# The order in which SP's queue issues the splits' returns and the weight loads, in a two-layer gated attention kernel

## What is computed

```
x = x + tanh(g_xattn[0]) * attention0(norm(x), ctx)   # 16 heads of 8, causal mask j < i
x = x + tanh(g_ffn[0])   * experts0(norm(x))          # 6 low-rank experts, best one, log of sum of exp
x = x + tanh(g_xattn[1]) * attention1(norm(x), ctx)   # 8 heads of 64
x = x + tanh(g_ffn[1])   * experts1(norm(x))          # 2 of 8 experts per batch, GELU, norm
```

## Time and profile before

| what | us |
|---|---|
| median of 3 runs | 203.16 (201.14 to 204.28) |
| the profiled execution | 203.85 |
| its span, first to last instruction | 201.8 |

### The profile page before, as it was taken

How to read it: one execution, slowest core, us unless ns; L and a number is a source line. 1 busy time by engine, 2 the same in 40 slices (tenths; PEclk the granted TensorE clock), 3 DMA queues, 4 the chain that set the end, 5 groups by cost and what they waited for, 6 DMA issues and landing times.

```text
span 201.8 us, 4473 instructions
## 1 busy us (share of the span) xinstructions
PE 182.0 (90%) x1575; PEld 130.8 (65%) x1575; DVE 145.3 (72%) x362; ACT 121.8 (60%) x315; POOL 103.8 (51%) x152
## 2 busy tenths in 40 slices
PE   7999786698999897998999998998999999999990
PEld 2677362455556555675686775857966959989980
DVE  2466695889998865279957689498789867747674
ACT  3558412854787685679769756496779954155240
POOL 6330000248655474277871785858958846282212
PEclk9999999979999999699999999999999999999998
DMA  5788999808300000000000000000160070708010
GB/s 132 229 254 162 302 190 236 159 26 158 58 8 2 4 3 3 0 0 3 0 0 2 5 0 0 3 0 0 21 220 0 5 232 3 224 18 248 8 52 29
DMA packets 14673, 15.13 MB, mean 75 GB/s; under 512 B 1703, under 2 KB 12044, under 8 KB 14652
## 3 DMA queue, kind: packets, MB, share of 16 engines
q1 hardware_dynamic: 14292, 14.75, 28.9%
q10 hardware_dynamic: 360, 0.10, 0.3%
HBM read 11.11 MB, written 3.67 MB: 73 GB/s over the span
## 4 chain that ended last, share of the span: by engine, by line
PE 54%; DVE 19%; DMA 7%; SPq 6%; POOL 6%; issue 3%; ACT 2%; POOLq 0%; DVEq 0%; ACTq 0%
PE PS L1288 6%; PE PS L1346 6%; PE PS L1336 5%; PE PS L1304 5%; DVE XH L733 5%; PE PS L1275 5%; PE PS L1261 4%; SPq L369 4%; PE PS L1152 4%; DMA POOLED<-qk_scr 3%; DVE MX L765 3%; PE PS L1316 3%; PE PS L1172 2%; PE PS L1047 2%; DMA CT<-in_ctxT 2%
## 5 line engine op out<-in xcount | busy, mean ns | idle before, releaser
L474 POOL TENSOR_TENSOR POOLED<-POOLED,RC 128x512 f32<-128x512 f32 x32 | 33.1, 1054 | 10.2 <-DVE RC L877 10.2
L765 DVE TENSOR_REDUCE MX<-PS 128x4 f32<-128x1024 f32 (+1 forms) x24 | 28.2, 1218 | 5.9 <-PE PS L1116 5.6
L661 ACT ACTIVATE POOLED<-PS,NM 128x256 f32<-128x256 f32 x64 | 29.4, 481 | 5.0 <-DVE NM L868 2.6
L463 POOL TENSOR_SCALAR_AFFINE_SELECT PT<-PT 128x512 f32<-128x512 f32 x16 | 10.3, 641 | 41.5 <-ACT PT L579 41.5
L579 ACT ACTIVATE PT<-PS 128x768 f32<-128x768 f32 x32 | 25.3, 809 | 6.5 <-PE PS L1133 5.3
L733 DVE TENSOR_SCALAR XH<-X,MV,RS 128x128 f32<-128x128 f32 x32 | 16.4, 552 | 8.0 <-POOL RS L432 8.0
L868 DVE TENSOR_REDUCE NM<-PS 128x4 f32<-128x1024 f32 x16 | 19.5, 1217 | 3.4 <-PE PS L1275 3.3
L431 POOL TENSOR_SCALAR VE<-MV 128x2 f32<-128x2 f32 x20 | 4.9, 245 | 30.0 <-DVE MV L718 16.9
L692 ACT ACTIVATE POOLED<-PS,BI 128x256 f32<-128x256 f32 x32 | 12.5, 474 | 11.5 <-PE PS L1336 9.7
L1275 PE MATMUL PS<-KT,VA 64*128 64x256 f32 x128 | 17.8, 399 | 0.1
L1288 PE MATMUL PS<-CST,POOLED 128*128 128x128 f32 x128 | 16.9, 275 | 0.0
(11 more groups left out here) (152 smaller groups left out, 400.3 us busy)
## 6 DMA issues: line engine op xcount, KB each, us to landing
POOLED<-in_w SPq DMA_DIRECT2D x8, 512.0 KB, 4.1
POOLED<-qk_scr SPq DMA_DIRECT2D x8, 384.0 KB, 5.8
qk_scr<-POOLED SPq DMA_DIRECT2D x8, 192.0 KB, 3.6
qk_scr<-POOLED SPq DMA_DIRECT2D x8, 128.0 KB, 4.5
W<-in_w SPq DMA_DIRECT2D x3, 256.0 KB, 4.0
BI<-in_bias SPq DMA_DIRECT2D x8, 66.0 KB, 3.8
qk_scr<-POOLED SPq DMA_DIRECT2D x8, 64.0 KB, 4.1
out_x<-X SPq DMA_DIRECT2D x4, 128.0 KB, 1.8
```

The source lines that it names most:

```text
L474: g_.tensor_tensor(pr, pr, RC1[:, n % 2, 2 * h:2 * h + 2].unsqueeze(2).to_broadcast([P, 2, S]), ALU.mult).then_inc(s_p1p, 1)
L661: last = a.activation(PR[n % 3][:, h, it, :], pair("sc", n)[:, h * 512 + it * S:h * 512 + (it + 1) * S], ACT.Exp, bias=NM1[:, n % 2, 2 * h ...
L765: v.tensor_reduce(MX0[:, b, it, :, hw * k:hw * (k + 1)], pair("S", n).rearrange("p (r h j) -> p r h j", r=2, h=hw), AXX, ALU.max, negate=T ...
```

## The change

Only the table `SP_ORDER` changes. No entry is added or removed.

- `w1:0` moves from behind `so:0:2` to behind `shift:1`.
- `si:1` moves up to directly behind `so:1:2`; `te` moves from there to behind `so:2:2`.
- `si:2` moves up to behind `te`, ahead of `vec` and `so:3:0`.
- `shift:0` stands behind `so:3:1`; `wo:0` behind it.
- `si:3` stands directly behind `so:3:2`, ahead of `shift:1`.

```
 SP_ORDER = table("""
-x:0 w0 c:0 w1:1 x:1 c:1 cm w1:2 x:2 one so:0:0 so:0:1 so:0:2 w1:0 c:2 si:0 so:1:0 so:1:1 so:1:2 te so:2:0 so:2:1
-si:1 so:2:2 vec so:3:0 shift:0 si:2 so:3:1 wo:0 so:3:2 shift:1 si:3 wo:1 shift:2 shift:3 w12:0 w12:1 w12:2 w12:3
-outd:0 outd:1 outd:2 outd:3
+x:0 w0 c:0 w1:1 x:1 c:1 cm w1:2 x:2 one so:0:0 so:0:1 so:0:2 c:2 si:0 so:1:0 so:1:1 so:1:2 si:1 so:2:0 so:2:1
+so:2:2 te si:2 vec so:3:0 so:3:1 shift:0 wo:0 so:3:2 si:3 shift:1 w1:0 wo:1 shift:2 shift:3 w12:0 w12:1 w12:2
+w12:3 outd:0 outd:1 outd:2 outd:3
 """)
```

## The result

| | median us | runs |
|---|---|---|
| before | 202.73 | 4, 201.14 to 204.28 |
| changed | 210.08 | 4, 209.79 to 211.11 |

The ratio is 1.040, 95% interval 1.032 to 1.048: slower, by 7.35 us. The two profiled executions are 203.85 and 211.11, their spans 201.8 and 209.0, so they show the same 7.2. The forecast was 208.3 in a range of 203.9 to 211.0. Single executions of one kernel differ by several us; ratios here leave out those over 1.5% above the fastest of their kernel, medians do not.

What follows compares the result with a forecast made beforehand. SP's queue was taken to bound the first 33 us, then VectorE's maxima and TensorE from 35.95 on. The terms 0 + 0 + 4.9 + 0.3 gave +5.2 us, forecast 208.3, range 203.9 to 211.0.

Steps and rivals of the forecast that it cites:

- Part 1: SP's queue at batch 1's return: si:1 goes out 1.1 us earlier, S:6 starts 1.2 us earlier, at 31.4.
- Part 2: Front of SP's queue: w1:0 leaving it gains 0 to 0.5 us before S:0; taken as nothing.
- Part 3: SP's queue behind si:2: shift:0 lands at 41.3, T:0:0 moves from 35.75 by +5.55 us, net +4.9.
- batch 0's pattern: SP's queue: work issued behind si:0 landed 7.8 to 8.8 us after it; shift:0 taken as 8.5 after si:2.
- half of vec's transfer: Queue ahead of shift:0: vec's 260 KB would add a little under 1 us; half left out of shift:0's landing.
- rival C: At T:0:0: the queue is longer, shift:0 lands at 44.8, net 8.4 us, time 211.8; chance 0.06.
- Given back: VectorE's maxima behind T:0:0: mx:8 already done, mx:9 follows 0.75 after T:0:0 and S:9, returning 0.65 us.
- Part 4: At T:4:0: shift:1 queues behind si:3, T:4:0 stands 0.5 to 1.5 us; cost taken as 0.3, bounds 0 and 1.
- The clock: TensorE after the new pause: low clock for a similar time, its phase moved; cost 0, bound +1 us.
- The sum: Whole kernel: 0 + 0 + 4.9 + 0.3 = +5.2 us on the span of 201.8, 208.3 forecast.

Runs made afterwards that it cites:

- experiment 2: The kernel before with shift:0 alone moved down, behind so:3:1: 207.74 us, ratio 1.023.
- experiment 5: The changed kernel with both shifts put ahead of the returns, shift:0 ahead of si:2 and shift:1 ahead of si:3: 202.22 us, ratio 0.995 to the kernel before.
- experiment 4: The kernel before with si:1 alone moved up, directly behind so:1:2: 203.47 us, ratio 1.001.
- experiment 3: The kernel before with w1:0 alone moved, behind si:3: 203.29 us, ratio 0.999.
- experiment 7: The changed kernel with shift:0 directly behind si:2, ahead of vec, so:3:0 and so:3:1: 206.75 us in one execution.
- experiment 1: The changed kernel with shift:0 alone put back ahead of si:2: median 207.3 us, too scattered for a ratio.
- experiment 10: The kernel before with shift:1 alone put behind si:3: 205.20 us, ratio 1.014.
- experiment 8: The changed kernel with ScalarE issuing both halves of each shift on its own queue: 208.55 us, ratio 1.029 to the kernel before.
- experiment 6: The changed kernel with shift:1 alone put ahead of si:3, shift:0 staying behind so:3:1: 210.17 us, ratio 1.038 to the kernel before.
- experiment 9: The changed kernel with 36 idle products on TensorE ahead of T:0:0: 208.71 us, ratio 1.031 to the kernel before.

## Why the prediction was right, and where its sizes were off

**The mechanism held.** SP's order moved shift:0 behind a wait and four entries' transfers (si:2, vec, so:3:0 and so:3:1), T:0:0 waited for it, and the gain of the early si:1 disappeared in that wait. Experiments 2 and 5 show this from both sides: the one entry, moved down in the kernel before, costs 4.4 us; the two shifts put back undo all of the loss.

**Part 1, si:1.** Forecast 24.05 and S:6 at 31.4. In the changed kernel it was 24.86, and S:6 followed mT:0 at 31.85 with no wait for the return; both go with si:0, which was 0.7 late; in experiment 4 it was 23.68 and 31.38. That the gain ends in the next wait was right.

**Part 2, w1:0.** At 0, which agrees with experiment 3 (ratio 0.999).

**Part 3, shift:0, mis-sized.** This term, +5.55 at T:0:0, measured +7.93 (43.68 less 35.75). Three pieces: si:2 went out at 33.82 instead of 32.85, for the chain si:0, si:1 had slid by 0.7 to 0.8 (+1.0); the issue was 3.95 after si:2, inside the 3.3 to 4.1 stated; and the landing was 9.7 after si:2 (37.77 + 5.77 less 33.82), not 8.5 (+1.2). The last write of so:3:1, right ahead of it, was issued at 36.78 and landed 6.5 us later, at 43.3, and shift:0 at 43.5. So the work ahead took longer than in batch 0's pattern. The half of vec's transfer that I had left out is up to 0.6 of that; where the rest comes from is open. Te is an unlikely source, as three of its five loads had landed within 0.8 us of si:2's issue. How the landing grows with what is put ahead is seen side by side, less 0.14 from landing to start: 6.7 us after si:2 with nothing between (experiment 7), 7.2 with so:3:1 between (experiment 2), 9.7 with vec, so:3:0 and so:3:1. (The remaining 0.14 is that step from landing to start.) T:0:0 at 43.68 is nearer to rival C's 44.8 than to my 41.3, though the late si:2 is part of that. In the cases with no more than so:3:1 between, the shift landed within 0.5 us of its return's second half: 39.5 against 39.7 (experiment 7), 39.7 and 39.4 (experiment 2), 50.6 and 51.0 (experiment 1), 50.4 and 50.1 (experiment 10).

**Given back, 0.65.** Measured 0.2: the second maxima group began at 37.12 before and at 44.86 now, +7.7. The products T:0:0 and S:9 ran at half the clock and took 1.2 us, not 0.75, which used up most of what I had counted.

**Part 4, si:3 ahead of shift:1, at 0.3.** In this kernel right: a wait of 0.65 with hT:1's wait behind it. It was right only because T:0:0 was so late. Experiments 10 and 1 give the entry's own price: 2.1 us in the order of before, and about 5 in the changed order (207.3 against 202.2, with the scatter of experiment 1). A term costed under the cover of another stall should have been named with its price without that cover.

**The clock, at 0.** Wrong in both directions. From 44.86 to T:4:0 the delay grew from 7.7 to 9.1 while the clock was 0.50 until 53, with the 0.65 of the second wait in it, and it is 8.5 at the first output product (51.92 before, 60.45 now). Then 1.4 came back at once: in the kernel before the clock was 0.51 from 80.8 to 83.8, in most of the query product of batch 0, and in the changed one it was at full speed there. Two chains of waits, before and changed:

```profile
82.77 0.87 PE PS L1172 x4
```

```profile
88.19 1.97 PE PS L1261 x8
90.16 0.45 PE PS L1172 x4
```

3.10 us against 1.97 for the same eight matmuls, and 0.87 against 0.45 for the transposes behind them. From there to the end the delay is 7.1 to 7.2. That stretch is not a mark of slow orders: of the twelve traces only before and experiment 3 have it (3.10 and 3.65 us for the query product, 1.97 in the other ten). Whether it comes with an order or with an execution is not shown.

**The sum.** 4.9 forecast at the second maxima group, 7.7 measured; +0.8 to the first output product; -1.4 at the query product; together 7.1 of the 7.2 found. I had 5.2. That the time still fell inside the range was luck: without the 1.4 that the query product gave back, which I had not foreseen, the 8.5 would have made 211.2 or more on the median, just past the upper end of 211.0.

The Trainium skill's section on queues, rings and completion order (DMA: Bandwidth & Descriptors) has descriptors taken in ring order on each engine; the copy of 8 KB that took 5.77 us in the changed kernel and 5.9 in experiment 7 agrees. The same page says under its heading that issuing engines are not separate DMA queues that starting DMAs on another engine saves only the sequencer's time. Experiment 8 agrees as far as the transfer goes, which took 4.1 and 5.9 us from ScalarE's own queue. But leaving SP's order saved more than the time of an issue, 5.5 us at T:0:0, since the copy no longer stood behind SP's waits.

## What to carry to other kernels

On an in-order queue, price a small transfer by what has been issued ahead of it and not by its size: list for each wait of a compute engine which DMA ends it, and what that DMA now stands behind. A transfer moved forward saves only down to the wait that it has itself (here for the landing of the writes), and the entries it passes can pay for it (in experiment 4, a wait of 1.9 us at T:0:0). Where two stalls are in series, undo them one by one and together before judging either: the second was worth 0 with the first in place (experiment 6) and about 5 us without it (experiment 1 against 5).

## What the runs showed of the hardware that was not expected

- The same copy of 8 KB took at most 2.4 us with no return going out ahead of it (experiment 1, T:0:0), 5.0 to 6.5 us behind a return in the same queue (the changed kernel and experiments 1, 2, 6, 7, 9 and 10), and 4.1 and 5.9 us from another queue while returns were under way (experiment 8).
- TensorE's granted clock fell to 0.50 during the pause of 8.5 us and stayed there for 9 us of work behind it (44 to 53; TensorE was busy for 3.78 of the first 5 us and for all of the next 5); after a sparser stretch in the kernel before it was low for 3.1 us. The length of the low stretch did not follow the length of the stall alone: it was 0.50 from 38 to 48 in experiment 2, with a stall of 4.3 us.
- A low-clock stretch of 3 us (80.8 to 83.8) was there in the kernel before and not in the changed one, and moved the time by 1.4 us with no change to the instructions there.
